# A graph convolution's rows kept feature-major: one product, ScalarE scaling in place, TensorE turning into the residual sum

## The reference

```python
h = x @ W
norm = dinv[src_f] * dinv[dst_f]
out = segment_sum(h[src_f] * norm[:, None], dst_f, num_segments=n) + conv_bias
mu = out.mean()
xc = out - mu
std = jnp.sqrt((xc * xc).mean())
y = xc / (std + EPS) * ln_weight + ln_bias
y = jnp.where(y >= 0, y, prelu_a * y)
...
x = x + y + attention
x = x + experts(layernorm(x))          # router: two of eight experts per node
```

## Time and profile before

| what | value |
| --- | --- |
| median of three runs | 1372.16 us |
| lowest and highest run | 1369.58 and 1375.01 us |
| the profiled execution: its span, from the first to the last instruction | 1377.2 us |
| busy: PE, DVE, POOL, ACT | 90%, 70%, 62%, 39% of the span |
| mean granted TensorE clock | 0.960 |

### The profile page before, as it was taken

One profiled execution on the slowest core, in us unless ns is written; L12 is line 12 of the kernel. 1 busy time (PEld: TensorE's weight loads), 2 busy tenths in 40 slices (PEclk: granted clock), 3 DMA queues, 4 the chain that ended last, 5 costly groups with the idle time before them and its releaser, 6 DMA issues. The chain is left out here.

```text
span 1377.2 us, 30864 instructions
## 1 busy us (share of the span) xinstructions
PE 1245.3 (90%) x8354; PEld 1106.3 (80%) x8355; DVE 962.4 (70%) x2966; ACT 539.3 (39%) x1443; POOL 854.3 (62%) x836
## 2 busy tenths in 40 slices
PE   4997688999899999999898797985799999999998
PEld 4984687887788888887787686873699999999997
DVE  8998787887888777778693288998444444444444
ACT  7707301222333333333311101446455555555553
POOL 1294677777777777777777202431376666666665
PEclk9999899999999999999999898995799999999999
DMA  7005333335666666789898400449244444444443
GB/s 245 0 0 183 111 106 103 107 105 172 194 194 199 198 191 202 207 246 277 260 288 261 144 1 16 138 155 318 64 77 66 68 71 69 72 69 70 71 69 42
DMA packets 138148, 186.89 MB, mean 136 GB/s; under 512 B 21438, under 2 KB 116468, under 8 KB 137916
## 3 DMA queue, kind: packets, MB, share of 16 engines
q0 software_dynamic: 43440, 90.29, 28.7%
q1 hardware_dynamic: 94604, 95.40, 21.8%
HBM read 153.16 MB, written 33.41 MB: 135 GB/s over the span
## 5 line engine op out<-in xcount | busy, mean ns | idle before, releaser
L740 POOL DMA_INDIRECT RG<-table,srci x484 | 477.3, 986 | 153.0 <-issue 149.4
L757 PEld LDWEIGHTS ps<-S_t,RG 128*128 128x128 f32 x1936 | 259.2, 196 | 39.0 <-DMA RG<-table,srci 28.6
L757 PE MATMUL ps<-S_t,RG 128*128 128x96 f32 x1936 | 266.4, 278 | 21.6 <-DMA RG<-table,srci 21.1
L780 PE MATMUL ps<-zrow,R 128*128 128x256 f32 (+1 forms) x784 | 221.1, 389 | 15.2 <-DMA zrow<-table 8.7
L2010 POOL DMA_INDIRECT out<-R,S_t x105 | 166.3, 1584 | 99.5 <-DVE R L1980 55.8
L1893 PE MATMUL ps<-R,RG 128*128 128x128 f32 x1680 | 207.3, 277 | 0.0
L1893 PEld LDWEIGHTS ps<-R,RG 128*128 128x128 f32 x1680 | 198.3, 194 | 0.4 <-issue 0.4
L1903 PE MATMUL ps<-R 128*128 x840 | 198.5, 379 | 0.0
L1014 DVE TENSOR_TENSOR R<-R,ps 128x245 f32 (+4 forms) x300 | 142.1, 474 | 73.7 <-PE ps L768 52.5
L1926 ACT ACTIVATE R<-ps,RG 128x128 f32<-128x128 f32 x420 | 120.0, 368 | 175.8 <-PE ps L1893 175.8
L1976 DVE TENSOR_TENSOR R<-ps,R 128x256 f32<-128x256 f32 x105 | 44.6, 425 | 200.8 <-PE ps L1903 200.8
(11 more groups left out here) (360 smaller groups left out, 1989.9 us busy)
## 6 DMA issues: line engine op xcount, KB each, us to landing
zrow<-table SPq DMA_DIRECT2D x384, 128.0 KB
RG<-table,srci POOLq DMA_INDIRECT x484, 3.3
ntable<-R SPq DMA_DIRECT2D x12, 516.0 KB
table<-RG SPq DMA_DIRECT2D x12, 512.0 KB, 2.9
out<-R SPq DMA_DIRECT2D x12, 512.0 KB, 3.2
R<-in_x SPq DMA_DIRECT2D x6, 896.0 KB, 11.7
R<-in_w SPq DMA_DIRECT2D x8, 514.0 KB, 6.4
slot<-in_x SPq DMA_DIRECT2D x32, 128.0 KB
```

Of the source, the lines that this page charges most:

```text
L740: nc.gpsimd.indirect_dma_start(out=grows[:, s, :], out_offset=None, in_=table, in_offset=bass.IndirectOffsetOnAxis(ap=srci[:, ND + q, c:c ...
L757: last = nc.tensor.matmul(window(q % 2)[:, h, :], grows[:, s, h * P:(h + 1) * P], S_t[:, q % 2, c, :], start=c == 0, stop=c == GC - 1)
L780: nc.tensor.matmul(psD[:, 0:D], adj[b % 2][0:n, j, :], zrow[0:n, i % ZR, :], start=j == 0, stop=j == T - 1).then_inc(z_used, 1)
```

## The change

The first loop takes the products the other way round: the weights are stationary, and spans of 512 nodes of `acc` are moving, so the rows stay feature-major. VectorE multiplies by `dinv`, now a row of numbers along the nodes that is the same on all partitions, and writes back into `acc`. The bias, the scales and the shifts become one number per partition. There is no second product. ScalarE computes for each span and half the positive part (`above`) and a scaled copy in place, VectorE joins them (`leak`), TensorE transposes each tile into PSUM (`gnn`), and VectorE adds it to the residual (`finish`). GpSimd does nothing in either loop. The row of `dinv` is made in the phase of the sums: TensorE turns `dinv`, ScalarE copies it, SP writes it to DRAM, and SP loads it 13 times, spread over all partitions, at the start of the node phase.

The core of the diff; semaphores and buffers are declared to match:

```diff
+SPAN = 512
+NSPAN = -(-N // SPAN)
-        cbias, lnw, lnb = (RG[:, k * D:(k + 1) * D] for k in (6, 7, 8))
+        cbias, lnw, lnb = (RG[:, 6 * D + k * KC:6 * D + (k + 1) * KC] for k in range(3))
+        dinv_row = R1[:, 0:NSPAN * SPAN]
...  phase of the sums: SP ahead of its row loads, and at its end; PE; ACT after two wipes
+                sp.wait_ge(dt_ok, 1)
+                sp.dma_start(dvec.rearrange("(t p) -> t p", p=P), dinv_turned).then_inc(late, 16)
...
+                for d_, s_ in ((cbias, a_cb), (lnw, a_lnw), (lnb, a_lnb)):
+                    sp.dma_start(d_, s_.rearrange("(k p) -> p k", p=P), allow_slow_non_contiguous=True).then_inc(late, 16)
+                nc.tensor.transpose(psD[0:T, 0:P], dinv[:, :], ident[:, :]).then_inc(dt_ps, 1)
+                act.wait_ge(dt_ps, 1)
+                act.activation(dinv_turned, psD[0:T, 0:P], ACT.Copy).then_inc(dt_ok, 1)
...  node phase, SP ahead of its stores
+                for c in range(NSPAN):
+                    sp.dma_start(dinv_row[:, span(c)], dvec[span(c)].unsqueeze(0).to_broadcast([P, span(c).stop - span(c).start]))\
+                        .then_inc(dr_in[c], 16)
...  TensorE
-                    for k in range(KC):
-                        last = nc.tensor.matmul(ps[t % 4][:, 0:D], acc[:, k, t * P:(t + 1) * P], gw[:, k, :],
+                def rows(c):
+                    if c >= 2:
+                        pe.wait_ge(y_ok, KC * (c - 1))
+                    for f in range(KC):
+                        for k in range(KC):
+                            last = nc.tensor.matmul(ps[(KC * c + f) % 4][:, 0:n], gw[:, k, f * P:(f + 1) * P],
+                                                    acc[:, k, span(c)], start=k == 0, stop=k == KC - 1)
-                pe.wait_ge(wx_ok, 1)
+                def gnn(t):
+                    pe.wait_ge(g_out, KC * (t * P // SPAN + 1))
                     if t >= 2:
-                        pe.wait_ge(v_ok, t - 1)
+                        pe.wait_ge(x_ok, t - 1)
                     for k in range(KC):
-                        last = nc.tensor.matmul(psW[t % 2][:, 0:D], acc[:, k, t * P:(t + 1) * P], wx[:, k, :],
+                        last = nc.tensor.transpose(psW[t % 2][:, k * P:(k + 1) * P], acc[:, k, t * P:(t + 1) * P], ident[:, :])
-                for s in range(T + 5):
+                for s in range(T + 3):
                     if s < T:
-                        scaled(s)
-                    if 0 <= s - 4 < T:
-                        flip(s - 4)
-                    if 0 <= s - 5 < T:
-                        logits(s - 5)
+                        gnn(s)
+                    if 0 <= s - 2 < T:
+                        flip(s - 2)
+                    if 0 <= s - 3 < T:
+                        logits(s - 3)
...  ScalarE (negative goes)
+                def leaky(c):
+                    for f in range(KC):
+                        i = KC * c + f
+                        if i >= 4:
+                            act.wait_ge(g_out, i - 3)
+                        act.activation(above[i % 4][:, 0:n], acc[:, f, span(c)], ACT.Relu, scale=y_scale[:, f:f + 1],
+                                       bias=y_shift[:, f:f + 1]).then_inc(g_in, 1)
+                        act.activation(acc[:, f, span(c)], acc[:, f, span(c)], ACT.Identity, scale=a_scale[:, f:f + 1],
+                                       bias=a_shift[:, f:f + 1]).then_inc(g_in, 1)
+                act.wait_ge(wx_ok, 1)
+                for c in range(2):
+                    leaky(c)
+                for s in range(T + 2):
+                    if s % 4 == 1 and s // 4 + 2 < NSPAN:
+                        leaky(s // 4 + 2)
+                    if 0 <= s - 2 < T:
+                        flipped(s - 2)
...  GpSimd: share_of and residual(t) for all tiles go
...  VectorE
-                    nc.vector.scalar_tensor_tensor(y_all[:, t, :], ps[t % 4][:, 0:D], dinv[:, t:t + 1], cbias, ALU.mult,
-                                                   ALU.add).then_inc(y_ok, 1)
+                    for f in range(KC):
+                        nc.vector.tensor_tensor(acc[:, f, span(c)], ps[(KC * c + f) % 4][:, 0:n], dinv_row[:, span(c)],
+                                                ALU.mult).then_inc(y_ok, 1)
+                def row_stats(c):
+                    for f in range(KC):
+                        last = nc.vector.bn_stats(ystats[:, f, c, :], acc[:, f, span(c)])
...
-                ch.done(nc.vector.tensor_scalar(aw, lnw, d2, None, ALU.mult))
-                ch.done(nc.vector.tensor_tensor(wx, gw, aw.unsqueeze(1).to_broadcast([P, KC, D]), ALU.mult))
+                ch.done(nc.vector.tensor_scalar(y_scale, lnw, d2, None, ALU.mult))
+                ch.done(nc.vector.tensor_scalar(y_shift, cbias, mu, None, ALU.subtract))
+                ch.done(nc.vector.tensor_tensor(y_shift, y_shift, y_scale, ALU.mult))
+                ch.done(nc.vector.tensor_tensor(y_shift, y_shift, lnb, ALU.add))
+                nc.vector.tensor_scalar(a_scale, y_scale, pre[:, :], None, ALU.mult)
+                ch.done(nc.vector.tensor_scalar(a_shift, y_shift, pre[:, :], None, ALU.mult))
                 v.sem_inc(wx_ok, 1)
+                def leak(c):
+                    for f in range(KC):
+                        i = KC * c + f
+                        v.wait_ge(g_in, 2 * i + 2)
+                        nc.vector.scalar_tensor_tensor(acc[:, f, span(c)], above[i % 4][:, 0:n], a1, acc[:, f, span(c)],
+                                                       ALU.mult, ALU.add).then_inc(g_out, 1)
+                def finish(t):
                     v.wait_ge(px_ok, t + 1)
+                    nc.vector.tensor_tensor(halved(o_all[:, t, :]), halved(psW[t % 2][:, 0:D]), o_tile(t),
+                                            ALU.add).then_inc(x_ok, 1)
-                for s in range(T + 4):
+                for c in range(2):
+                    leak(c)
+                for s in range(T + 2):
+                    if s % 4 == 1 and s // 4 + 2 < NSPAN:
+                        leak(s // 4 + 2)
                     if s < T:
-                        shifted(s)
...
+                        finish(s)
+                    if 0 <= s - 1 < T:
+                        x_stats(s - 1)
+                    if 0 <= s - 2 < T:
+                        x_stats_joined(s - 2)
```

More of the change, by code:

```diff
@@ L1283, in build @@
         over(phase)
[L1286 to L1289, removed]
+        tot2 = small[:, 24:26]
+        y_scale, y_shift = small[:, 48:48 + KC], small[:, 52:52 + KC]
+        a_scale, a_shift, a1 = small[:, 54:54 + KC], small[:, 56:56 + KC], small[:, 20:21]
+        above = [slot[:, 2 * k:2 * k + 2, :].rearrange("p s f -> p (s f)") for k in range(2)] + [
+            RG[:, k * 4 * D:k * 4 * D + SPAN] for k in range(2)]
         wrg = RG[:, 3 * D:3 * D + KC * NX].rearrange("p (k e) -> p k e", k=KC)
@@ L1359, in build @@
             whole = semaphore(phase, "r_total_sums")
[L1360 to L1365, removed]
+            dr_in = [semaphore(phase, f"r_inverse_roots_in{c}") for c in range(NSPAN)]
+            wx_ok = semaphore(phase, "r_scales_ready")
+            px_ok = semaphore(phase, "r_gnn_turned")
+            g_in = semaphore(phase, "r_gnn_scaled")
+            g_out = semaphore(phase, "r_gnn_ready")
             x_ok = semaphore(phase, "r_x1_ready")
@@ L1396, in build, with span @@
             psF = [ps[2], ps[3]]
-            shift, turned, minus = slot, zrow[:, 0:2, :], zrow[:, 2:6, :]
+            turned = zrow[:, 0:2, 0:D]
+            def span(c):
+                return slice(c * SPAN, min(c * SPAN + SPAN, N))
             psL, psR, psC8, psI = ps[4], ps[5], ps[6], ps[7]
@@ L1467, in _ @@
                 last.then_inc(g_ps, 1)
-                for t in range(4, T):
-                    rows(t)
+                for c in range(2, NSPAN):
+                    rows(c)
                 for n in range(2):
@@ L1584, in _ @@
                 nc.gpsimd.tensor_copy(code16, code_i).then_inc(ready, 1)
-                def residual(t):
-                    pool.wait_ge(v_ok, t + 1)
-                    nc.gpsimd.tensor_tensor(o_tile(t), o_tile(t), halved(shift[:, t % 4, :]), ALU.add).then_inc(xa_ok, 1)
-                for t in range(T):
-                    residual(t)
                 def join_weights(h):
@@ L1632, in _ @@
                         ch.done(last)
-                    last = row_stats(t)
+                    last = row_stats(c)
                 ch.done(last)
-                full = 1.0 / (N * D)
+                full = 1.0 / D
                 pm, tm = small[:, 32:34], small[:, 34:36]
                 means, variances = (small[:, 32:36].rearrange("p (a b) -> p a b", b=2)[:, :, k] for k in range(2))
-                ch.done(nc.vector.bn_aggr(pm, stats[:, 0:T - 1, :].rearrange("p t s -> p (t s)")))
-                ch.done(nc.vector.bn_aggr(tm, stats[:, T - 1, :]))
-                v.wait_ge(sh_ok, 2)
-                ch.done(nc.vector.tensor_tensor(tot2, means, share_of, ALU.mult))
```

(5 more changed lines are left out.)

80 lines of the change are left out of this document (25 added, 55 removed).

## The result

| | before | after |
|---|---|---|
| median, us (range) | 1373.59 (1369.58 to 1375.44) | 1389.29 (1386.32 to 1393.42) |
| ratio to before, 95% interval | | 1.0112 (1.0079 to 1.0145) |
| profiled execution: span, us | 1377.2 | 1385.8 |
| granted TensorE clock, second loop | 1.00 | 0.50 |

The changed kernel is 15.7 us slower; 1387 (1367 to 1396) was predicted. The profiled spans are only 8.6 apart because the phase of the sums, which is the same work up to a row of small loads, ended 6.2 us earlier in the one execution than in the other (789.92 and 783.67 for the first product behind it). Between the kernels of this study that start lies anywhere from 781 to 790, so stages are compared from it.

What follows compares the result with a forecast made beforehand. TensorE was taken to bound both loops, the new second one at clock 0.50. First loop +2.5, scales -0.6, second loop +12.8 gave +14.7 us: 1392 on the profiled 1377.2, 1387 on the median 1372.16, range 1367 to 1396.

Steps and rivals of the forecast that it cites:

- What bounds the old loop: Second loop before the change: TensorE sets the pace at 1.53 us per tile at full clock, VectorE level with it.
- First loop, scales, after the loop: Stages around the second loop: first loop +2.5 us, mean and scales -0.6 us, chain behind the second loop unchanged.
- The clock: New second loop: TensorE stays at clock 0.50 throughout, 1.71 us per tile, against 0.89 at full clock.
- the second: Clock evidence before the loops: L1526's short matmuls keep TensorE busy 16.55 of 17 us, yet the clock stays 0.50.
- The second loop's sum: Second loop, opening to last logits: 94.3 us, including 388 TensorE passes at 0.213 (82.6); +12.8 us against before.
- the wait behind `leaky`: Second loop, once per span: logits wait because `leaky` precedes `flipped`, 3.7 against 3.4 us, 0.3 x 11 = 3.3.
- The end of the loop: Second loop's end: last tile's copy and hand-offs 1.4 us; VectorE's norm chain done by the last logits, then L1724.
- The first rival: Second loop: the clock rises to full, four tiles take 5.7 us, 1368 us; without waits 1355; chance 0.19.
- ScalarE as the bound: Second loop rival: at 1.0 us or more per operation, `leaky` holds logits 1.5 us per span, 1400 us; chance 0.07.

Runs made afterwards that it cites:

- interleaved: Changed kernel with ScalarE's four operations of a span issued one per tile behind that tile's copy, VectorE's two `leak` two tiles apart: 1376.78 us.
- the grouped loop: The second loop in the changed kernel's own order, `leaky` once per span with ScalarE's four operations together; with nothing added: 1389.29 us.
- the grouped kernel with the burst only: Changed kernel plus matmuls useless to the output, 16 ahead of the second loop and 6 at each of two early steps, none per tile: 1386.05 us.
- the interleaved one with the burst only: Changed kernel, ScalarE's operations one per tile, plus useless transposes ahead of the second loop and at its second and third step: 1351.93 us.
- the grouped loop with the extra matmul: Changed kernel plus one f32 matmul of 128 columns per tile that does nothing for the output, none added ahead of the loop: 1402.60 us.

## Why the prediction was right, and where its sizes were off

**What bounds the old loop: right.** TensorE at 1.53 per tile, and VectorE level with it only because GpSimd's share slows its finishing addition: without GpSimd the tile stays at 1.53 and VectorE idles.

**First loop, scales, after the loop: right.** +2.1 for +2.5, -0.5 for -0.6, 0 for 0. VectorE's statistics end 832.95 - 829.42 = 3.5 after TensorE (829.42 is the end of its last product), where 3.9 was expected.

**The clock: its level right, and it decided; the reason given for it isn't borne out.** 0.50 from 833.2, when the first loop's products were over, to 990.2. The prediction weighed against the last of the earlier trace rows and took the second, because the new loop's passes are so short and its transposes so few; the changed loop did stay down. But this work doesn't have to run there: the same eight passes per tile, interleaved, stayed at 1.00 for 61 us once a burst had raised it, and at 0.50 for the whole loop without the burst in the profiled run. The same instructions in another order hold either level. What the profiles show of the cause is the order of events: the grouped loop fell back behind every burst (three kernels), the interleaved one behind none (three kernels), one profiled run each; the mean clocks of their other runs agree. At 1.00 TensorE stood idle for more of the time in the loop that fell: from 842 to 858 it was busy 10.07 of 16.00 us in the grouped kernel with the burst only, and 12.16 in the interleaved one with the burst only; later it was busy 15.78 of 20.00 in the grouped loop with the extra matmul and 17.37 of 20.00 in the interleaved one with the burst. At 0.50 both are busy nearly throughout (57.17 of 60.00, 58.00 of 58.00) and neither rose in those profiled runs. No run varies the idle time alone, so why the one loop falls and the other doesn't stays open.

The Trainium skill, "TensorE: Matmul & The Clock Gate", Part 4: PE-mode transpose, has it that the full clock doesn't engage for transposes. The earlier trace rows spoke against that, and the runs do too: the clock rose to 1.00 during bursts of nothing but transposes (four kernels; at 839.8 in the fastest), and a loop whose long passes are all transposes kept it for 61 us. The transposes here are of f32; the page's timings are of bf16.

**The second loop's sum: right as a sum, by two errors that cancel.** That is luck. The prediction put TensorE's passes at 0.213 each, 1.71 per tile, and the wait behind `leaky` at 0.3 per span. Measured are 1.60 and 0.79.

The pairs of transposes are 0.46 and 0.42, near 2 x 0.213, but the four logits take 0.72, 0.18 each: they were costed as if they streamed as long as a transpose, where L1472 and L1473 had only bounded them from above. The earlier trace rows had a nearer price: from 859.95 to 860.32 four logits take 0.37 at the full clock, 0.09 each, not the 0.11 read there, and twice that is 0.18. So 388 passes x 0.213 = 82.6 stand against 48.5 tiles x 1.60 = 77.6: -5.0.

The wait was taken as the difference of two totals, 3.7 against 3.4. The chain of ScalarE, from one copy's start to the logits behind the next, takes 892.03 - 888.52 = 3.51. But TensorE's passes fill only 2.94 of it, up to 891.04 + 0.42 = 891.46, since they are shorter than costed and fewer than 16 of them are left when the copy starts (2.94 / 0.20 = 14.7): 0.57. The logits that waited then take 892.98 - 892.03 = 0.95 in place of 0.72. Together that is 0.80 per span, and all that follows on TensorE is late by as much. It comes behind nine spans, not eleven: the short last span makes no wait, and the first shows as a wait at the loop's head, where the finishing addition of the second tile stands behind VectorE's `leak`:

```profile
847.49 0.63 PE L1510 MATMUL ps<-ident,R 128*128 128x128 f32 x2
849.85 0.66 PE L1502 MATMUL ps<-ident,R 128*128 128x128 f32 x2 [1.73 <-DVE R L1704]
```

By the interleaved kernel, which has neither wait, that head costs 1.96. In sum 9 x 0.79 + 1.96 = 9.1 stand against 3.3: +5.8. With the -5.0 that is +0.8, and the stage shows +0.6. Taking the loop's tile and its waits from one added-up term hid both.

**The end of the loop: a small miss.** Not the logits but VectorE's norm chain is last there: ScalarE's square root (L1584) stands behind the last copies, VectorE is idle 1.73 us for it, and L1749 follows at the end of that chain.

**The rivals.** The first rival's price, 1368 at the full clock, rested on 5.7 us per four tiles in the grouped order. The stretches at 1.00 took 6.0 to 6.5, level with the old loop's 6.12: by these few, the change as it stands would have won little even if the full clock had held. No run holds it there throughout. What the rival named as its ideal, 1.08 per tile on VectorE with no waits, 1355 us, is what the interleaved order with the clock up reached: 1.055 and 1351.93. ScalarE as the bound fell: its operations are 0.70 apart (0.71 predicted), and halving them left TensorE's 1.60.

**Where the change's gain went.** From after to the best kernel the loop goes from 94.9 to 59.5: 9.1 by the order (85.8 interleaved at 0.50) and 26.3 by the clock, one profiled run each. The interleaved kernel's run of 1355.01, without a burst, is some 3 us above the best. The change did take 0.70 us per tile of TensorE's work at the full clock away (1.53 to 0.83: in the kernel with the burst only the transposes of one tile start at 875.69, those of the next at 876.52); it lost it to the clock, which was 1.00 in the middle of the old loop and 0.50 here, and to a group of ScalarE operations that stood ahead of a copy on which TensorE waits.

## What to carry to other kernels

Before taking dense matmuls out of a loop, cost what is left at both levels of TensorE's clock, and read from the granted clock what the engine did just before the loop; a short burst of transposes in its head can be worth more than the change (26 us in the interleaved loop, with the first finishing addition 6.5 us after the scales both with and without it), or next to nothing where the loop falls back behind it (94.9 to 92.6 with a burst of matmuls in the grouped one). Work that an engine does for later tiles is dealt out one piece per tile, behind the piece that another engine waits for: the same four operations cost TensorE 0.79 us per span as a group and nothing when spread, both at 0.50. When two terms of a sum share an engine, check each against a row of its own, since their errors can cancel.

## What the runs showed of the hardware that was not expected

- The interleaved loop, with the same instructions but for the burst ahead of it, was seen at either clock for its whole length: 0.50 for the loop's 86 us in one profiled run without the burst, 1.00 for 61 us in one with it. Without the burst, a run of 1355.01 us stands beside three of 1375 to 1379.
- f32 logits matmuls of 8 columns, each behind a full weight load, are 0.18 us apart at clock 0.50 and 0.09 at 1.00; a pair of 128-column transposes takes 0.42 to 0.46 and 0.22 to 0.25.
- One f32 matmul of 128 columns per tile cost 0.53 us at 0.50, more than the pair of transposes of the same width, (8.11 - 6.40) / 4 = 0.43.
